# A 16-head attention stage on one core: the softmax shift moved into the score product, and the first norm's affine moved to GpSimd

## The reference, cut to what matters

```python
# step 1: cross attention, 16 heads of 16 channels
q = split_heads(x @ Wq, 16); k = split_heads(ctx @ Wk, 16); v = split_heads(ctx @ Wv, 16)
scores = einsum('bhqd,bhkd->bhqk', q, k) / sqrt(16)
attn = softmax(scores, axis=-1)
x = x + (einsum('bhqk,bhkd->bhqd', attn, v) merged) @ Wo       # norms and residuals around it
# step 2: feed-forward with quantised levels
h = layernorm(x, ln1_g, ln1_b)
h = act_quant(h)            # round(h * 127 / max|h|) per token
h = h @ ternary(w1) + b1; h = gelu(h); h = layernorm(h, ln2_g, ln2_b)
x = x + act_quant(h) @ ternary(w2) + b2
```

## Time and profile before

| | |
|---|---|
| three runs | 419.77, 414.97, 419.32 us; median 419.32 |
| span of the profiled execution | 414.9 us; its time as a run is not listed apart |
| busy | PE 335.8, DVE 305.9, ACT 263.8, POOL 183.8 us |
| attention stage | from 45.9 us to about 171 us |
| a turn in it | 7.50 us, the same from turn 2 to turn 15, but for turn 7, which is 0.96 us longer |

### The profile page before, as it was taken

One profiled execution on the slowest core, in us unless ns is written; L12 is line 12 of the kernel. 1 busy time (PEld: TensorE's weight loads), 2 busy tenths in 40 slices (PEclk: granted clock), 3 DMA queues, 4 the chain that ended last, 5 costly groups with the idle time before them and its releaser, 6 DMA issues.

```text
span 414.9 us, 9157 instructions
## 1 busy us (share of the span) xinstructions
PE 335.8 (81%) x3093; PEld 236.8 (57%) x3093; DVE 305.9 (74%) x1025; ACT 263.8 (64%) x567; POOL 183.8 (44%) x207
## 2 busy tenths in 40 slices
PE   2999589998999999823678787779488999999864
PEld 2777467776776777502345555446265666666421
DVE  2798735777889988676997999985436777787751
ACT  1565335466445455735788898886668888888520
POOL 2114300212212465139997899982005555445520
PEclk9999989999999999955979999999889999999986
DMA  7499999979653640000000000000001222222000
GB/s 251 122 283 303 299 217 214 257 136 266 128 105 88 130 42 2 1 0 0 2 1 2 0 2 2 2 0 2 0 14 28 38 53 53 46 46 39 28 25 25
DMA packets 43869, 33.68 MB, mean 81 GB/s; under 512 B 19888, under 2 KB 39728, under 8 KB 43696
## 3 DMA queue, kind: packets, MB, share of 16 engines
q1 hardware_dynamic: 43824, 33.11, 32.7%
HBM read 24.71 MB, written 8.39 MB: 80 GB/s over the span
## 4 chain that ended last, share of the span: by engine, by line
PE 55%; DVE 18%; issue 13%; ACT 7%; POOL 4%; DMA 2%; SPq 1%; DVEq 0%; POOLq 0%; ACTq 0%
PE PS L1461 5%; PE PS L1238 5%; PE PS L1227 4%; DVE sm L741 4%; PE PS L1296 4%; PE PS L1451 4%; PE PS L1218 4%; PE PS L1217 4%; PE PS L1157 4%; PE PS L1257 3%; PE PS L1446 3%; PE PS L1424 3%; ACT pT L991 2%; DVE sm L713 2%; PE PS L1414 2%
## 5 line engine op out<-in xcount | busy, mean ns | idle before, releaser
L991 ACT ACTIVATE pT<-PS 128x512 f32<-128x512 f32 x64 | 36.6, 596 | 50.8 <-PE PS L1218 50.5
L606 DVE TENSOR_REDUCE negm<-PS 128x4 bf16<-128x512 f32 x64 | 42.3, 683 | 15.6 <-PE PS L1227 15.5
L435 POOL TENSOR_TENSOR sm<-sm,mhalf 128x1 f32<-128x1 f32 x16 | 11.3, 708 | 83.8 <-DVE sm L638 83.8
L451 POOL TENSOR_TENSOR kst<-kst,rows 128x1024 f32<-128x1024 f32 x16 | 37.6, 2351 | 8.1 <-ACT kst L1059 8.0
L1103 ACT ACTIVATE lnT<-PS,Atok 128x128 f32<-128x128 f32 x128 | 36.4, 368 | 3.7 <-DVE lnb L849 2.0
L1336 PE MATMUL PS<-identf,w2f 128*128 128x128 f32 x128 | 19.2, 297 | 20.6 <-ACT w2f L1048 20.6
L1218 PE MATMUL PS<-identb,negm 128*128 128x128 bf16 x256 | 35.6, 222 | 0.0
L465 POOL TENSOR_TENSOR kst<-kst,rows 128x1024 f32<-128x1024 f32 x14 | 33.1, 2363 | 0.0
L1238 PE MATMUL PS<-pT,vx 128*32 128x128 f32 x512 | 27.3, 287 | 5.0 <-ACT pT L991 5.0
L1336 PEld LDWEIGHTS PS<-identf,w2f 128*128 128x128 f32 x128 | 15.2, 151 | 24.9 <-ACT w2f L1048 19.6
L1461 PE MATMUL PS<-wd,xT 128*128 128x392 f32 x64 | 27.0, 548 | 1.8 <-DVE rest L885 1.8
(11 more groups left out here) (220 smaller groups left out, 977.7 us busy)
## 6 DMA issues: line engine op xcount, KB each, us to landing
scr_q<-qpart SPq DMA_DIRECT2D x8, 384.0 KB, 3.9
scr_k<-kpart SPq DMA_DIRECT2D x8, 384.0 KB, 4.7
X<-in_x SPq DMA_DIRECT2D x8, 256.0 KB, 4.5
CTXT<-in_ctxT SPq DMA_DIRECT2D x8, 256.0 KB, 4.7
vx<-in_ctx SPq DMA_DIRECT2D x16, 128.0 KB, 3.0
out<-rest SPq DMA_DIRECT2D x16, 128.0 KB, 1.7
rows<-in_rows SPq DMA_DIRECT2D x1, 1544.0 KB, 8.9
qst<-scr_q SPq DMA_DIRECT2D x8, 192.0 KB, 4.4
```

The source lines that it names most:

```text
L451: gp.tensor_tensor(n2[q.slot], n2[q.slot], ln2g, ALU.mult).then_inc(b_g2, 1)
L606: v.tensor_reduce(negm[f.slot % 2][:, 4 * hg:4 * hg + 4], PS[:, 2 + hg % 2, :].rearrange("p (h k) -> p h k", h=4), AX_X, ALU.max, negate=T ...
L991: s.activation(pT[:, hg, :], PS[:, hg % 2, :], ACT.Exp, scale=float(DH0) ** -0.5).then_inc(a_e, 1)
```

## The change

1. The stacks grow from 96 rows to 104 (`SHIFT`). Rows 96 to 103 of `kst` hold one-hot rows: row 96+i is 1 for the heads i and 8+i. GpSimd writes them once per slot (`place_ones`), two copies of 8 x 1024 for each of the first four groups of the projections, between two powers.
2. The negated maxima go to columns 96 to 111 of a zeroed `negm`. TensorE turns them (`turn_maxima`, two products per batch, eight heads each) into rows 96 to 103 of PSUM; ScalarE copies each to eight heads of the query stack (`shift_rows`, 8 x 1024). `shifted` is then a single product of 104 rows per head; the 16 products with `negm` of each batch are gone.
3. For batches 0 to 13, GpSimd does the norm's affine (`normed`, three instructions of 128 x 256) and the levels (one more), instead of L641, L653 on VectorE and `level` on ScalarE. Batches 14 and 15 keep the old way.
4. The order of the turns is rewritten on TensorE, VectorE and ScalarE. The statistics of `d` come first on VectorE, the query copies stand between `exp(3)` and the copy of `yT` on ScalarE.

```diff
-        negm = [sb(f"negm{i}", [128, H0], BF16) for i in range(2)]
+        negm = [sb(f"negm{i}", [128, STACK + 16], BF16) for i in range(2)]
@@ GpSimd, turn_p
+            def place_ones(i):
+                for half in range(2):
+                    step(gp.tensor_copy(kst[i][STACK:SHIFT, 8 * half:8 * half + 8, :],
+                                        identf[STACK:SHIFT, STACK:SHIFT].unsqueeze(2).to_broadcast([8, 8, S])))
                     gp.tensor_tensor(rs[f.slot % 2][:], ve[f.slot % 2][:], mhalf[:, 0:GP], ALU.pow).then_inc(p_rs, 1)
+                    pool.wait_ge(p_rs, f.b + 1)
+                    if f.b < 4:
+                        place_ones(f.b)
+                    elif f.b < 6:
+                        step(gp.memset(negm[f.b - 4][:], 0.0))
@@ GpSimd, turn_a
+            def normed(d):
...
+                gp.tensor_scalar(t1[:], X[:, d.b, :], z[:, 5:6], z[:, 3:4], ALU.add, ALU.mult).then_inc(l_p, 1)
+                pool.wait_ge(l_p, 3 * d.b + 1)
+                gp.tensor_tensor(t1[:], t1[:], ln1g, ALU.mult).then_inc(l_p, 1)
+                pool.wait_ge(l_p, 3 * d.b + 2)
+                gp.tensor_tensor(u1[d.b], t1[:], ln1b, ALU.add).then_inc(l_p, 1)
...
-                    pool.wait_ge(l_c, d.b * 7 + 4)
+                    if d.b < NB - 2:
+                        normed(d)
+                    else:
+                        pool.wait_ge(l_c, l_links(d.b) + 4)
                     gp.tensor_tensor(X[:, d.b, :], X[:, d.b, :], b2r, ALU.add).then_inc(l_xb, 1)
+                    if d.b < NB - 2:
+                        pool.wait_ge(l_c, l_links(d.b) + 5)
+                        gp.tensor_scalar(u1[d.b], u1[d.b], z[:, 6:7], MAGIC, ALU.mult, ALU.add).then_inc(l_u, 1)
                     if 9 <= d.b < 12:
                         scale_rows(d.b - 9)
@@ VectorE, turn_a
+                if d:
+                    ln1_stats(d)
+                if f:
+                    take_max(f, 0)
+                    take_max(f, 1)
                 if c:
                     normalise(c)
...
                 if f:
                     take_max(f, 2)
                     take_max(f, 3)
                 if d:
-                    ln1_scale(d, centred)
+                    ln1_scale(d)
@@ VectorE, the start of ln1_scale
+                if d.b < NB - 2:
+                    dve.wait_ge(l_p, 3 * d.b + 3)
+                else:
+                    ln1_affine(d)
@@ ScalarE, turn_a, behind exp(0), exp(1) and the copies of vx and yT2
+                if b:
+                    exp(2)
+                    exp(3)
+                if f:
+                    shift_rows(f, 0)
+                    shift_rows(f, 1)
+                if b:
+                    act.wait_ge(a_pv, b.b * 4 + 4)
+                    done(act, a_t4, b, 0)
+                    s.activation(yT[:], PS[:, 5, :], ACT.Copy).then_inc(a_yT, 1)
+                if f and f.b in (5, 6):
+                    weight_sum(f.b - 5)
+                if e and e.b >= NB - 2:
                     level(e)
@@ ScalarE, the copy
+            def shift_rows(at, half):
+                act.wait_ge(a_nt, 2 * at.b + half + 1)
+                s.activation(qst[at.slot][STACK:SHIFT, 8 * half:8 * half + 8, :],
+                             PS[STACK:SHIFT, 4, 256:384].unsqueeze(1).to_broadcast([8, 8, S]), ACT.Copy).then_inc(a_bc, 1)
@@ TensorE
                 def shifted(hg):
-                    pe.wait_ge(a_mx, b.b * 4 + hg + 1)
+                    pe.wait_ge(a_bc, b.b * 2 + hg // 2 + 1)
                     done(pe, a_e, b, 0, 4, hg - 1)
                     for j in range(4):
...
-                        t.matmul(block, kst[b.slot][0:STACK, h, :], qst[b.slot][0:STACK, h, :], start=True, stop=False)
-                        last = t.matmul(block, negm[b.slot % 2][:, h:h + 1].to_broadcast([128, 128]), identb[:],
-                                        start=False, stop=True)
+                        last = t.matmul(PS[:, hg % 2, j * 128:(j + 1) * 128], kst[b.slot][0:SHIFT, h, :],
+                                        qst[b.slot][0:SHIFT, h, :], start=True, stop=True)
+                def turn_maxima(half):
+                    pe.wait_ge(a_mx, f.b * 4 + 2 * half + 2)
+                    if half == 0:
+                        pe.wait_ge(a_v, f.b + 1)
+                    else:
+                        pe.wait_ge(a_bc, f.b * 2 + 1)
+                    t.matmul(PS[0:SHIFT, 4, 256:384], negm[f.slot % 2][:, 8 * half:8 * half + SHIFT], identb[:],
+                             start=True, stop=True).then_inc(a_nt, 1)
```

More of the change, by code:

```diff
@@ L429, in scale_rows @@
                 gp.tensor_scalar(row, row, by, None, ALU.mult).then_inc(s_sr, 1)
+            def normed(d):
+                z = sm1[d.slot % 2]
+                if d.b == 0:
+                    for i in range(SETS):
+                        pool.wait_ge(p_stored[i], SETS_STORED[i])
+                    pool.wait_ge(p_tr, NG)
+                pool.wait_ge(l_r, d.b + 1)
+                if d.b:
+                    pool.wait_ge(l_p, 3 * d.b)
+                gp.tensor_scalar(t1[:], X[:, d.b, :], z[:, 5:6], z[:, 3:4], ALU.add, ALU.mult).then_inc(l_p, 1)
[3 more added lines that the diff above has]
+                gp.tensor_tensor(u1[d.b], t1[:], ln1b, ALU.add).then_inc(l_p, 1)
             def turn_a(_f, _b, _c, d):
@@ L597, in sum_weights, with start @@
                 wlink(v.tensor_tensor(wg[:, KC:2 * KC, :], wg[:, KC:2 * KC, :], wg[:, 2 * KC:3 * KC, :], ALU.add))
-            cl = Chain(dve, l_c, 7)
+            class Links(Chain):
+                def start(self, at):
+                    self.base, self.n, self.per = l_links(at.b), 0, l_links(at.b + 1) - l_links(at.b)
+            cl = Links(dve, l_c, 0)
             def take_max(f, hg):
@@ L637, in ln1_centre, with ln1_affine @@
                 dve.wait_ge(l_c, var)
+                if d.b < NB - 2:
+                    v.tensor_scalar(z[:, 5:6], z[:, 0:1], -1.0, None, ALU.mult)
                 v.tensor_scalar(z[:, 2:3], z[:, 1:2], 1.0 + EPS, EPS * EPS, ALU.mult, ALU.add).then_inc(l_w, 1)
-                if d.b == 0:
-                    dve.wait_ge(s_rows, 16)
-                return cl.mark(v.scalar_tensor_tensor(out=t1[:], in0=X[:, d.b, :], scalar=z[:, 0:1], in1=ln1g,
-                                                      op0=ALU.subtract, op1=ALU.mult))
-            def ln1_scale(d, centred):
+            def ln1_affine(d):
                 z = sm1[d.slot % 2]
-                if d.b == 0:
-                    for i in range(SETS):
-                        dve.wait_ge(p_stored[i], SETS_STORED[i])
-                    dve.wait_ge(p_tr, NG)
+                dve.wait_ge(s_rows, 16)
+                dve.wait_ge(l_p, 3 * (NB - 2))
+                centred = cl.mark(v.scalar_tensor_tensor(out=t1[:], in0=X[:, d.b, :], scalar=z[:, 0:1], in1=ln1g,
+                                                         op0=ALU.subtract, op1=ALU.mult))
                 dve.wait_ge(l_r, d.b + 1)
@@ L787, in _ @@
             spreads(first, None, 1)
-            ln1_scale(before_last, ln1_centre(before_last, ln1_stats(before_last)))
+            ln1_stats(before_last)
+            ln1_scale(before_last)
             update(last)
-            centred = ln1_centre(last, ln1_stats(last))
+            ln1_stats(last)
             turn_b(2, *peeled(2, NB, 4, 9))
-            ln1_scale(last, centred)
+            ln1_scale(last)
             for tau in range(3, NB + 8):
@@ L998, in turn_a @@
                         columns(Turn(0, 0, 0))
-                    exp(2)
+                if f:
+                    act.wait_ge(a_vm, f.b + 1)
+                    done(act, a_pv, f, -1, 4)
+                    s.activation(vx[f.slot % 2][:, :, 0:DH0], PS[:, 4, 0:256].rearrange("p (h e) -> p h e", h=H0),
+                                 ACT.Copy).then_inc(a_v, 1)
                 if c:
@@ L1240, in pv @@
                     last.then_inc(a_pv, 1)
+                if f:
+                    pe.wait_ge(a_ld[f.slot], LOADED * (f.used + 1))
+                    for_max(0)
+                    for_max(1)
+                if b:
+                    shifted(0)
+                    shifted(1)
                 if c:
@@ L1250, in turn_a @@
                         up(Turn(1, 1, 0))
+                if b and b.b == NB - 1:
+                    columns(Turn(0, 0, 0))
                 if f:
-                    pe.wait_ge(a_ld[f.slot], LOADED * (f.used + 1))
-                    for_max(0)
-                    for_max(1)
+                    for_max(2)
                     done(pe, a_v, f, 0)
+                    done(pe, a_bc, f, 0, 2)
                     for kc in range(KC):
@@ L1259, in turn_a @@
                     last.then_inc(a_vm, 1)
-                if b:
-                    shifted(0)
-                    shifted(1)
-                    if b.b == NB - 1:
-                        columns(Turn(0, 0, 0))
                 if c:
@@ L1278, in turn_a @@
                     pv(0)
-                if f:
```

(9 more changed lines are left out.)

45 lines of the change are left out of this document (18 added, 27 removed).

## The result

The changed kernel takes 419.61 us in the median of 20 runs (417.21 to 422.68), the kernel before, on the same chip, 416.63 (413.34 to 419.77). The ratio is 1.0072 with a 95% interval of [1.0051, 1.0092]: slower by 0.7%, a small difference that the interval still keeps apart from none, where I had forecast 1.5% faster. The profiled span grows from 414.9 to 417.3 us.

What follows compares the result with a forecast made beforehand. TensorE bounds attention, VectorE close behind. Turns +9.2, GpSimd's queue -1.4 and -0.3, tail +0.4: net 7.9, taken as 7.5, less fills 1.2: 6.3 us gained, 408.6 against the span, 413.0 against the median; range 407.5 to 421.

Steps and rivals of the forecast that it cites:

- a return in GpSimd's queue: Turns 12 to 16: GpSimd's longer queue gives back 1.4 us of the gain, and 0.3 more for hand-overs.
- the end: Tail after `hidden(0)`: its end and ScalarE's `columns(1)` copy come earlier, a gain of 0.4 us.
- The hold of the norm by the fills: Projections: GpSimd's fills hold VectorE's norm by 0.3 us a group, 1.2 in all.
- the rule: Skill page: the shared pair of ports goes to the first comer, VectorE or GpSimd, for its whole instruction.
- My own other end: Projections: by the page, a fill of 2.33 us holds the norm 1.7 a group, 6.9 in all; time 418.7.
- The turns to turn 12: Attention up to turn 12: 9.2 us gained with the first turns' 1.7; the result's table gives -7.5 from turn 2.
- the plain turn: Turns 2 to 5 and 8: 6.45 us instead of 7.50, a gain of 1.05 each.
- The ring: Plain turns: loop of waits from TensorE through ScalarE's exponentials, both query copies and `yT` copy; sum 6.39, taken as 6.45.
- The first turns: Turn 1 some 2 us shorter by the new order, but limited by batch 2's stack DMA: gain 1.7 us.
- The way to `hidden(0)`: Start of turn 12 to `hidden(0)`: GpSimd's queue makes it 36.0 us, against 34.6 before.
- the moved wait: Rival, attention: the wait moves to ScalarE and GpSimd in full; plain turn 6.9, time 417.7, or 419 to 421; chance 0.18.
- The long fills: Rival, projections: every power waits behind two long fills; 433 us, or 420 by the scaling's row; chance 0.12.

Runs made afterwards that it cites:

- `own_bank`: Changed kernel with late fills, plus the second half of the turned maxima in PSUM bank 6; ratio 0.9954 to the kernel before.
- the new order shows: `yT_order`: late fills, halved scalings, `yT` copied between the query copies, against the changed kernel; 0.9829 to before. `order_alone`, that order only: 1.0031. Plain turns 6.34 in both.

## Why the prediction was wrong

Its frame held: gains in the turns, a cost in the projections, a return in GpSimd's queue. Four terms were mis-sized, all to the same side: by 3.0, 3.3, 1.5 and 1.6 us, in the order below and by the table's rows; the end gave 0.3 back.

1. **The hold of the norm by the fills** (1.2 taken, 4.05 measured) is the step that turned a tie into a loss: without it the ratio is 0.9985, no gain either, and the missing gain lies in the other three. Against the other profiles the hold is some 3.1 us. The length of a fill was right (1.034 for 0.9), and so was that the queue hides it. Wrong was 0.3 a group for the hold: it was 0.9, 2.1, 0 and 1.0 in the four rounds. In groups 0 and 1 the fill and the norm are released by the same power, so they always meet; I had worked the overlap out for a later group alone and then carried it to all four. I had also let one row, L595, speak against the rule. My own other end, the rule with long fills, gave 6.9.
2. **The turns to turn 12** (-7.5 taken, -4.2 measured), above all the plain turn (6.45 taken, 6.97 measured). The ring was a right one, through both copies and `yT`, but as far as the second turning TensorE's own work takes as long, which `own_bank` showed and I had not summed. The ring's pieces were each a little short: TensorE's first part 2.75 for 2.59, `exp` 0.55 for 0.49, twice, a hand-over of 0.14 behind the first query copy for 0.04, and 1.04 from the second copy to `yT`, where I had counted 0.89. That is 0.5 a turn; a sum of eight pieces on one ring needs each one's full step. Behind it TensorE would have allowed 6.34, as the new order shows, less than the 6.7 of busy time that I had left it. Besides, I had counted turn 8 as plain. It has the first ternary step (in the trace of before at 112.11 us) and gained 0.4, not 1.05.
3. **The first turns** (-1.7 taken, -0.2 measured). I had left turn 0 as it was; its waits for the query copies made it 5.85 us instead of 5.00. Turn 1 fell from 8.60 to 7.58, where I had 1.7 less: I took TensorE's products at full speed, and after these waits it was at the lower clock, with 1.75 us for the values projection and 0.85 for eight scores, which are 0.92 and 0.45 else. Since the start varies by a microsecond between profiles, the size of this term is uncertain by as much.
4. **The way to `hidden(0)`** (1.7 taken, 3.3 measured). GpSimd's queue was less long than I had summed: the power of batch 12 comes 25.4 us after the start of turn 12 (135.3 to 160.69), where I had 27.2, since a multiply-add takes 0.547; the norm of batch 13 is through at 169.62. The step that failed is that this queue would set `hidden(0)`: that comes at 173.33 and waits for TensorE, which in turns 15 and 16 still has the new order's wait for `yT`, now without other work to fill it, and a lower clock. I had looked at one engine's queue and not at the chain of those two turns. From projection to projection, turns 12 to 14 are 1.2 us longer than before and the rest 0.2; what is left of the 3.3 is the place of a turn's first scores in the new order, which stands with the opposite sign in the row of turn 2.

Of the rivals, the moved wait (417.7 to 421) came nearest: plain turn 6.9, GpSimd's return 4. Its reasons were not those measured: multiply-add and copy were cheaper than it said, and it had no more than 1.2 for the fills. The long fills didn't happen. The range, to 421, held the time, but by luck of its base: I had added it to the 419.3 of three runs, and the 20 runs give 416.63. Counted from there it would have ended at 418.3, below the 419.61 measured.

## What to carry to other kernels

A short instruction put on GpSimd can hold up what VectorE has to do while it runs, above all when one semaphore releases both; place it where VectorE's next step is far, and check the meeting in every group. When work moves onto an engine's loop, order the copies by who waits for them: here two exchanges gave 0.6 us in each of four plain turns, more than the change itself, though turns 6 and 7 took most of it back. When a queue of work moves to an idle engine, add up its busiest turns, and then ask of the step that you want early what else it waits for.

## What was not expected of the hardware

- A query copy from 8 partitions took 1016 ns for 1024 columns, as the one from 128 partitions (1000): here the few partitions saved nothing.
- GpSimd needed 547 ns for a two-operation multiply-add of 128 x 256, less than for a product of two tiles (724), but 2.85 us for the scaling of 1024 columns in place, which is 5.2 times as long for four times the columns.
- The same level took 480 ns alone and 1.37 us when a 1.21 us VectorE step on the weights had begun ahead of it; a fill pair 2.13 or 3.07.
